# Another order of all engines, with rings of ten and eight buffers, in a fused state-space and local-attention kernel

## The chip, the cores and the metric

The kernel runs on one core of a Trainium2 chip. The metric is the device time of one execution in microseconds, lower is better. The engines are TensorE (PE; PEld is its weight loading), VectorE (DVE), ScalarE (ACT), GpSimd (POOL) and SyncE (SP), which issues all DMAs. Each runs its own instruction stream in order, and the streams meet through semaphores.

## What is computed

From x of 8 sequences x 256 tokens x 128 features, a layer norm gives xn. Two branches start from it:

```python
xn = _layernorm(x)
s = mamba_block(xn)           # projection, causal convolution of 4 taps, silu, softplus,
                              # scan hc = a*hc + b over 256 tokens for 256 x 16 states, output projection
for i in range(6):            # the other branch
    x = attn_layer(shift_tokens(x), Wqkv[i], ...) + x   # 16 heads of 64, windows of 32 that look one window back
    x = ffn_layer(shift_tokens(x), ...) + x             # layer norm, a * gelu(gate), 128 -> 2*341 -> 128
g = silu(x)
out = x0 + s * g              # x0: the kernel's input
```

In attention, q and k are normalised by head, scaled and rotated; the softmax runs over 64 positions of two windows.

## The kernel before

Everything stays in on-chip memory. After a start phase (layer norm, transposes, constants) the main phase treats the attention branch as 48 steps, s = 8 * layer + sequence. A step's attention is cut into eight units of q and k (`qk`, half the tokens x 4 heads; line 623), four of values (`value`, line 639) and four groups of heads (`scores` lines 660 and 668, `values_out` line 702). Its way through the engines:

- TensorE `qk(s,u)` -> ScalarE `square` (line 979) -> VectorE `rotate` (two multiplications, line 1307) and `sum_squares` (line 1314) -> after all eight: `guard_q` (line 1321), ScalarE `guess_q`, VectorE `norm_q` (line 1330).
- GpSimd `rotate_sum` (line 1584, adds the two products into the ring AB of NAB slots) and `normalise` (line 1595) -> TensorE `turn` (four transposes, line 648) -> ScalarE `copy_qk` (line 988).
- TensorE `scores` -> VectorE `softmax` (lines 1337, 1340) -> ScalarE `expo` (line 995) -> VectorE `sum_p` (line 1350) -> GpSimd `normalise_p` (line 1602) -> TensorE `turn_p` (line 680) -> ScalarE `copy_p` (line 1003) -> TensorE `values_out` -> ScalarE `copy_o`.
- For a pair of sequences: `w_out` (line 719), `res_attention`, `mean_x` (line 726), `center` (VectorE, line 1366), `square_x` (ScalarE, sqx), `var_x` (line 732), `norm_x`, `w_gelu` (line 745), `gelu`, `w_gate` (line 758), `gate`, `w_down` (line 767), `res_ff`.

The state-space branch takes one sequence ("batch") every six steps; its operations have names with z_ and are spread over eleven steps. `z_x` (line 776), `z_tap`, `z_conv` (VectorE, line 1403: six shifted multiply-adds, and a small addition), `z_silu`, `z_dbc`, `z_dup` (line 804), `z_softplus`, `z_delta` make its inputs, and `z_g` (line 785) its gate. Then sixteen chunks j of 128 rows each: a DMA spreads rows (`replicate`), ScalarE makes the decay into the single PSUM bank M (`z_decay`, line 1164), GpSimd makes the input product (`z_bu`, line 1629) in the ring hb of NH slots, VectorE scans (`z_scan`, line 1417), GpSimd multiplies by C (`z_hc`, line 1640), and TensorE sums four chunks (`z_sum`, line 822). `z_gate`, `z_out` and `z_state` end the batch.

Each operation is a Python function with its waits inside, and returns at once when its step does not exist, is odd (pair operations) or is not a multiple of six (z_ operations). Every engine's function has one loop, `for i in STEADY` (i from -2 to 46), whose body is a list of calls with lags, as `z_scan(i - 5, 6)`. That hand-written list is the order of that engine: what has lag 5 comes, for a batch that starts at step s, in iteration s + 5. Behind the loops stand lists for the last step and the tail. At the switch to the next layer, `rotate_sum` of units 6 and 7 also makes rotation tables (line 1575), and SP loads the next weights (`next_qk`, `next_v`, `other_weights`).

PSUM banks are shared: the bank of R alternates between `qk`/`value` units, T takes all transposes, X scores and outputs, C0 the pair's work, M the z_ work, Y the sums. Who may write T, X and M after whom is worked out by `befores` from T_ORDER, X_ORDER and M_ORDER (lines 53 to 62), which must repeat TensorE's or ScalarE's order:

```python
            def rotate_sum(s, u):
                ...
                if n >= NAB:
                    pool.wait_ge(tr_full, n - NAB + 1)
...
            def z_bu(s, j):
                ...
                if n >= NH:
                    pool.wait_ge(zy_full, (n - NH) // ZSUM + 1)
```

Of the kernel before, what the change touches and what calls it, by code (L numbers as in the profile page):

```python
# [40 lines left out]
LAST = STEPS - 1  # L41
LAST_B = STEPS - BSTEP
LAST_Z = 16 * (STEPS // BSTEP - 1)
NAB = 9
NREP = 4
NH = 9
# [9 lines left out]
X_ORDER = [("values_out", 3, 1, 1), ("scores", 0, 0, 1), ("scores", 1, 0, 1), ("values_out", 0, 0, 1),  # L56
           ("scores", 2, 0, 1), ("values_out", 1, 0, 1), ("scores", 3, 0, 1), ("values_out", 2, 0, 1)]
M_ORDER = [("z_x", 0, -2, 6), ("z_out", 0, 9, 6), ("z_dbc", 0, 1, 6), ("z_dup", 0, 1, 6), ("z_g", 0, 4, 6),
           ("z_decay", 8, 6, 6), ("z_decay", 14, 8, 6), ("z_decay", 5, 5, 6), ("z_decay", 9, 6, 6),
           ("z_decay", 15, 8, 6), ("z_decay", 3, 4, 6), ("z_decay", 10, 6, 6), ("z_decay", 11, 7, 6),  # L60
           ("z_decay", 4, 4, 6), ("z_decay", 0, 3, 6), ("z_decay", 6, 5, 6), ("z_decay", 1, 3, 6),
           ("z_decay", 12, 7, 6), ("z_decay", 13, 7, 6), ("z_decay", 2, 3, 6), ("z_decay", 7, 5, 6)]
# [240 lines left out]
def main_phase(nc, t, k, R2, T, C0, X, M, Y):  # L303

    with ExitStack() as ctx:
# [142 lines left out]
        def _(sp):  # L448
# [105 lines left out]
            for i in STEADY:  # L554
                replicate(i - 6, 6)
                next_qk(i, 1)
                next_qk(i, 2)
                spread(i, 0)
                replicate(i - 3, 1)
                next_v(i, 0)  # L560
                next_qk(i, 3)
                spread(i, 1)
                replicate_bc(i - 3, 0)
                replicate_bc(i - 3, 1)
                next_qk(i + 1, 0)
                replicate(i - 3, 2)
                replicate_bc(i - 3, 2)
                replicate_bc(i - 3, 3)
                replicate(i - 2, 0)
                replicate(i - 6, 7)  # L570
                spread(i, 2)
                replicate_bc(i - 3, 4)
                spread(i, 3)
                arrange_x(i + 1)
                replicate(i - 5, 5)
                replicate(i - 4, 4)
                replicate(i - 3, 3)
                next_v(i, 1)
# [17 lines left out]
        def _(pe):  # L596
# [1254 lines left out]
```

## Time and profile before

| what | value |
|---|---|
| median of 3 runs | 1792.14 us (1791.08 to 1795.57) |
| profiled execution, its own time | 1786.7 us |
| its span | 1784.9 us |
| TensorE busy | 1691.1 us, 95% |
| VectorE busy | 1555.8 us, 87% |
| GpSimd busy | 1426.6 us, 80% |
| ScalarE busy | 1257.4 us, 70% |
| DMA | 113.13 MB, mean 63 GB/s |

The profile is that of one execution. An engine's busy time is the union of its instructions; ends of matmuls are modelled, and of pipelined ones they overlap the next start. Idle time in front of an instruction is put down to what released it last. In the timeline, rows give start and length in us, engine, line, operation, tiles (out<-in) with their shapes, and how many instructions are merged; idle time before them stands in brackets.

### The profile page before, as it was taken

Reading aid. Unit: us, or ns where it says so; the run is one execution under the profiler, and the core shown is the slowest. Engines: PE = TensorE matmul, PEld = TensorE weight load, DVE = VectorE, ACT = ScalarE, POOL = GpSimd, SP = SyncE. Lnnn points to the kernel's source line nnn. Section 1 sums busy time; section 2 is a strip of 40 time slices with the busy share of each in tenths; the row PEclk is TensorE's granted clock in tenths of the full one; section 3 lists DMA queues with packets and bytes.
Section 4 is the critical chain, followed back from the end, with each engine's and each line's share of the span. In section 5 each row is a group of like instructions: output and inputs, shape, how many; then the busy total and the mean of one; then the engine's idle time right before and its main releaser. Section 6 shows DMA issues by size and latency. Waiting matters only on the chain.

```text
span 1784.9 us, 73875 instructions
## 1 busy us (share of the span) xinstructions
PE 1691.1 (95%) x30944; PEld 983.4 (55%) x30944; DVE 1555.8 (87%) x2724; ACT 1257.4 (70%) x2328; POOL 1426.6 (80%) x1264
## 2 busy tenths in 40 slices
PE   3789999999999999999999999999999999999976
PEld 1355555555555655555555555555555555555542
DVE  5768999889989899899988999898998899989856
ACT  3566686776876777866867768667678677786665
POOL 1677888977888887888889878897888888798862
PEclk9999999999999999999999999999999999999999
DMA  4013233131312422132331423214131332213230
GB/s 112 22 40 72 50 88 81 38 91 44 89 30 55 111 66 47 36 74 69 82 72 26 89 55 75 77 37 94 46 80 29 82 85 64 50 37 69 53 93 24
DMA packets 94054, 113.13 MB, mean 63 GB/s; under 512 B 42318, under 2 KB 59484, under 8 KB 93724
## 3 DMA queue, kind: packets, MB, share of 16 engines
q1 hardware_dynamic: 93724, 108.41, 25.7%
q8 instruction: 246, 4.03, 1.0%
q14 instruction: 84, 0.69, 0.1%
HBM read 19.22 MB, written 1.05 MB: 11 GB/s over the span
## 4 chain that ended last, share of the span: by engine, by line
PE 62%; DVE 15%; POOL 9%; issue 8%; ACT 3%; DMA 1%; SPq 1%; POOLq 0%; DVEq 0%; ACTq 0%
PE bank L623 12%; PE bank L648 8%; PE bank L702 8%; PE bank L639 7%; PE bank L719 6%; PE bank L668 5%; PE bank L680 4%; DVE qn L1307 3%; PE bank L745 3%; DVE qc L1307 3%; POOL AB L1595 2%; POOL AB L1584 2%; PE bank L758 2%; DVE ssq L1314 2%; POOL hb L1629 2%
## 5 line engine op out<-in xcount | busy, mean ns | idle before, releaser
L1584 POOL TENSOR_TENSOR AB<-qc,qn 128x512 f32<-128x512 f32 x384 | 487.0, 1274 | 105.2 <-DVE qn L1307 103.2
L1595 POOL TENSOR_TENSOR AB<-AB,rinv 128x512 f32<-128x512 f32 x384 | 411.4, 1094 | 34.1 <-DVE rinv L1330 34.1
L623 PE MATMUL bank<-wqkv,XT 128*128 128x512 f32 x768 | 381.3, 599 | 5.2 <-DVE qn L1307 5.1
L1602 POOL TENSOR_TENSOR Pb<-Pb,p_rden 128x512 f32<-128x512 f32 x192 | 200.4, 1044 | 139.4 <-DVE p_rden L1351 137.4
L988 ACT ACTIVATE qkT<-bank 128x512 f32<-128x512 f32 x384 | 228.8, 596 | 109.1 <-PE bank L648 107.2
L979 ACT ACTIVATE sq<-bank 128x512 f32<-128x512 f32 x384 | 228.4, 595 | 95.7 <-PE bank L623 95.6
L1314 DVE TENSOR_REDUCE ssq<-sq 128x8 f32<-128x512 f32 x384 | 258.3, 673 | 9.9 <-ACT sq L979 9.2
L1307 DVE TENSOR_TENSOR qc<-bank,rt 128x512 f32<-128x512 f32 x384 | 258.6, 673 | 8.4 <-ACT sq L979 5.4
L1307 DVE TENSOR_TENSOR qn<-bank,rt 128x512 f32<-128x512 f32 x384 | 261.5, 681 | 0.0
L702 PEld LDWEIGHTS bank<-PT,V 64*64 64x64 f32 x12288 | 197.2, 135 | 97.4 <-issue 89.3
L648 PE MATMUL bank<-ident,AB 128*128 128x128 f32 x1536 | 242.7, 281 | 5.3 <-ACT qkT L988 2.7
L648 PEld LDWEIGHTS bank<-ident,AB 128*128 128x128 f32 x1536 | 173.7, 141 | 124.9 <-issue 82.2
L702 PE MATMUL bank<-PT,V 64*64 64x32 f32 x12288 | 218.1, 220 | 7.3 <-ACT PT L1003 3.6
L1003 ACT ACTIVATE PT<-bank 128x512 f32<-128x512 f32 x192 | 114.0, 594 | 153.2 <-PE bank L680 150.7
L639 PE MATMUL bank<-wqkv,XV 128*128 128x512 f32 x384 | 192.4, 603 | 6.0 <-DVE qn L1307 6.0
L1337 DVE TENSOR_REDUCE mx<-bank 128x8 f32<-128x512 f32 x192 | 131.4, 684 | 71.8 <-PE bank L668 71.1
L1417 DVE TENSOR_TENSOR_SCAN hb<-bank,hb 128x256 f32<-128x256 f32 x256 | 161.2, 671 | 29.5 <-ACT bank L1164 29.5
L719 PE MATMUL bank<-OT,wo 128*128 128x512 f32 x384 | 182.1, 597 | 0.0
L1629 POOL TENSOR_TENSOR hb<-rep,BC 128x512 f32<-128x512 f32 x128 | 162.9, 1279 | 17.7 <-PE bank L822 7.9
L623 PEld LDWEIGHTS bank<-wqkv,XT 128*128 128x128 f32 x768 | 127.9, 192 | 79.9 <-issue 70.2
L668 PE MATMUL bank<-qkT 64*32 64x64 f32 x12288 | 164.3, 222 | 2.5 <-issue 2.4
L995 ACT ACTIVATE Pb<-Pb 128x512 f32<-128x512 f32 x192 | 120.8, 629 | 62.5 <-DVE Pb L1340 62.3
(141 smaller groups left out, 2531.5 us busy)
## 6 DMA issues: line engine op xcount, KB each, us to landing
V<-V SPq DMA_DIRECT2D x672, 64.0 KB, 2.0
rep<-du SPq DMA_DIRECT2D x64, 512.0 KB, 4.8
wqkv<-in_Wqkv SPq DMA_DIRECT2D x36, 256.0 KB, 3.3
XV<-XT SPq DMA_DIRECT2D x96, 64.0 KB, 2.1
wo<-in_Wo SPq DMA_DIRECT2D x6, 512.0 KB, 5.3
BC<-BC SPq DMA_DIRECT2D x8, 256.0 KB
w<-in_W SPq DMA_DIRECT2D x6, 341.0 KB, 4.5
BC<-BC SPq DMA_DIRECT2D x8, 128.0 KB
```

The costliest lines, as they stand in the source:

```text
L623: pe.matmul(R[u % 2][:], XT[:, s % NB, (u % 2) * P:(u % 2 + 1) * P], wqkv[:, (u // 2) * 512:(u // 2 + 1) * 512], start=True, stop=True).th ...
L639: pe.matmul(R[n % 2][:], XV[:, q % 2, s % 2, tl, :], wqkv[:, c:c + 512], start=True, stop=True)\
L648: mm = pe.transpose(T[:, c * P:(c + 1) * P], AB[:, (8 * s + u) % NAB, c * P:(c + 1) * P], ident[:])
L668: mm = pe.matmul(SB[w * WIN:(w + 1) * WIN, odd, col:col + 2 * WIN], qkT[p0:p0 + DH, g % 2, c, WIN + tok:2 * WIN + tok], qkT[p0:p0 + DH, g ...
L702: mm = pe.matmul(o_bank(s)[DH * odd:DH * (odd + 1), tl, c * P + w * WIN:c * P + (w + 1) * WIN], V[r, w, h0:h0 + DH], PT[r, g % 2, 2 * odd ...
L719: mm = pe.matmul(c_bank("w_out", s), wo[:, k, :], flat(OT[:, k]), start=k == 0, stop=k == 7)
L979: act.activation(sq[:, u % 2, :], R[u % 2][:], ACT.Square).then_inc(sq_done, 1)
L988: act.activation(qkT[:, g % 2, :, WIN + tl * P:WIN + (tl + 1) * P], T.rearrange("p (c t) -> p c t", c=4), ACT.Copy).then_inc(qkT_done, 1)
L1307: ins = dve.tensor_tensor(out if z == 0 else out[:, :, :, ::-1, :], src, tab, ALU.mult)
L1314: dve.reduce_sum(ssq[:, 8 * u:8 * u + 8], sq[:, u % 2, :].rearrange("p (h d) -> p h d", d=DH), AX_X)\
L1584: pool.tensor_tensor(AB[:, n % NAB, :], qc[:, u % 2, :], qn[:, u % 2, :], ALU.add).then_inc(rs_done, 1)
L1595: pool.tensor_tensor(o, o, r, ALU.mult).then_inc(nm_done, 1)
```

## The change

All five lists of the steady loops are reordered, X_ORDER and M_ORDER with them; NAB goes from 9 to 10 and NH from 9 to 8. No operation's body changes. Some calls change their lag, that is, cross the edge of an iteration: `values_out(·, 3)` 1 to 0, `z_sum(·, 0)` 5 to 4, `z_gate` 9 to 8, `z_silu` -1 to 0, scans 2, 10 and 13 to one more, `z_bu` 3, 10, 11, and `z_hc` 0, 3, 4, 5, 8, `arrange_x` -1 to -2, and `next_qk` 1 to 3 from i to i + 1. Three calls of the last step's lists go, since the loop now makes them. The core of the diff (of SP, ScalarE and GpSimd what the texts speak of):

```diff
-NAB = 9
+NAB = 10
 NREP = 4
-NH = 9
+NH = 8
...
-X_ORDER = [("values_out", 3, 1, 1), ("scores", 0, 0, 1), ("scores", 1, 0, 1), ("values_out", 0, 0, 1),
-           ("scores", 2, 0, 1), ("values_out", 1, 0, 1), ("scores", 3, 0, 1), ("values_out", 2, 0, 1)]
+X_ORDER = [("scores", 0, 0, 1), ("scores", 1, 0, 1), ("values_out", 0, 0, 1), ("scores", 2, 0, 1),
+           ("values_out", 1, 0, 1), ("scores", 3, 0, 1), ("values_out", 2, 0, 1), ("values_out", 3, 0, 1)]
...
@@ SP
+                arrange_x(i + 2)
...
-                arrange_x(i + 1)
...
+                next_qk(i + 1, 1)
+                next_qk(i + 1, 2)
+                next_qk(i + 1, 3)
                 replicate(i - 4, 4)
...
@@ TensorE
             for i in STEADY:
+                turn(i, 0)
                 value(i, 2)
-                turn(i, 0)
-                values_out(i - 1, 3)
                 turn(i, 1)
                 value(i, 3)
                 scores(i, 0)
+                z_x(i + 2)
                 turn(i, 2)
+                z_out(i - 9)
                 qk(i + 1, 0)
-                qk(i + 1, 1)
-                turn(i, 3)
-                z_x(i + 2)
-                z_sum(i - 5, 0)
-                z_out(i - 9)
                 z_dbc(i - 1)
                 w_out(i - 2, 0)
+                turn(i, 3)
+                qk(i + 1, 1)
+                z_g(i - 4)
                 scores(i, 1)
                 turn_p(i, 0)
                 qk(i + 1, 2)
-                w_out(i - 2, 1)
+                turn(i, 4)
                 w_gelu(i - 3, 0)
                 values_out(i, 0)
+                turn(i, 5)
+                qk(i + 1, 3)
                 z_dup(i - 1)
-                turn(i, 4)
-                qk(i + 1, 3)
                 w_gelu(i - 3, 1)
-                turn(i, 5)
                 qk(i + 1, 4)
-                z_g(i - 4)
+                w_gelu(i - 3, 2)
+                w_out(i - 2, 1)
+                scores(i, 2)
+                qk(i + 1, 5)
+                turn_p(i, 1)
                 w_out(i - 2, 2)
-                w_gelu(i - 3, 2)
-                scores(i, 2)
-                turn_p(i, 1)
-                qk(i + 1, 5)
+                w_gate(i - 3, 0)
                 qk(i + 1, 6)
-                w_gate(i - 3, 0)
                 turn(i, 6)
                 values_out(i, 1)
                 turn(i, 7)
+                w_out(i - 2, 3)
                 w_gate(i - 3, 1)
-                w_out(i - 2, 3)
                 qk(i + 1, 7)
-                w_gate(i - 3, 2)
                 scores(i, 3)
                 turn_p(i, 2)
+                w_gate(i - 3, 2)
                 mean_x(i - 2)
                 value(i + 1, 0)
+                z_sum(i - 7, 2)
+                values_out(i, 2)
+                var_x(i - 2)
+                w_down(i - 3)
+                turn_p(i, 3)
                 z_sum(i - 6, 1)
-                w_down(i - 3)
-                z_sum(i - 7, 2)
+                z_sum(i - 4, 0)
                 z_sum(i - 8, 3)
-                var_x(i - 2)
-                values_out(i, 2)
-                turn_p(i, 3)
                 value(i + 1, 1)
+                values_out(i, 3)
...
-            values_out(LAST - 1, 3)
...
-            z_sum(LAST_B, 0)
...
@@ VectorE
             for i in STEADY:
-                z_gate(i - 9)
+                z_scan(i - 7, 10)
+                z_scan(i - 4, 2)
+                z_scan(i - 8, 13)
                 res_ff(i - 4)
                 softmax(i, 0)
-                z_scan(i - 5, 5)
                 z_scan(i - 8, 14)
                 z_scan(i - 6, 8)
+                z_state(i - 9)
+                z_conv(i + 2)
                 sum_p(i, 0)
+                sum_squares(i + 1, 0)
                 rotate(i + 1, 0)
-                sum_squares(i + 1, 0)
-                z_conv(i + 2)
-                z_scan(i - 6, 9)
                 softmax(i, 1)
                 rotate(i + 1, 1)
-                z_scan(i - 8, 15)
+                rotate(i + 1, 2)
                 sum_squares(i + 1, 1)
-                rotate(i + 1, 2)
+                z_scan(i - 3, 0)
+                z_scan(i - 5, 5)
...
                 softmax(i, 3)
                 center(i - 2)
+                gate(i - 3, 2)
+                sum_p(i, 3)
+                sum_squares(i + 1, 6)
                 sum_squares(i + 1, 7)
                 guard_q(i + 1)
-                sum_p(i, 3)
-                z_scan(i - 3, 0)
                 rotate(i + 1, 7)
                 norm_q(i + 1)
-                z_scan(i - 6, 10)
-                z_scan(i - 3, 1)
-                z_scan(i - 5, 6)
-                z_scan(i - 7, 12)
-                z_scan(i - 3, 2)
-                z_scan(i - 7, 13)
                 norm_x(i - 2)
                 z_scan(i - 4, 4)
+                z_scan(i - 5, 6)
+                z_gate(i - 8)
+                z_scan(i - 7, 12)
                 z_scan(i - 5, 7)
+                z_scan(i - 3, 1)
@@ GpSimd
                 normalise(i, 0)
                 normalise(i, 1)
-                z_hc(i - 8, 12)
+                z_hc(i - 6, 4)
+                z_bu(i - 5, 7)
                 normalise(i, 2)
                 normalise(i, 3)
-                z_bu(i - 4, 4)
+                z_hc(i - 7, 9)
+                z_hc(i - 4, 1)
+                z_hc(i - 8, 12)
+                rotate_sum(i, 7)
                 normalise(i, 4)
-                z_bu(i - 7, 11)
+                z_hc(i - 8, 13)
+                normalise_p(i, 0)
+                z_bu(i - 7, 12)
                 normalise(i, 5)
-                z_hc(i - 6, 6)
-                z_hc(i - 5, 3)
-                rotate_sum(i, 7)
-                normalise_p(i, 0)
-                normalise(i, 6)
...
-            z_hc(LAST_B, 3)
```

## Rows read from the trace of the kernel before

**Rows 1.** The page: busy time, share and instructions of each engine.

```profile
PE 1691.1 (95%) x30944; PEld 983.4 (55%) x30944; DVE 1555.8 (87%) x2724; ACT 1257.4 (70%) x2328; POOL 1426.6 (80%) x1264
```

**Rows 2.** The page: the chain that ended last, by engine.

```profile
PE 62%; DVE 15%; POOL 9%; issue 8%; ACT 3%; DMA 1%; SPq 1%; POOLq 0%; DVEq 0%; ACTq 0%
```

**Rows 3.** Stages: window, length, busy of PE, PEld, DVE, ACT, POOL, clock, DMA.

```profile
56.00:188.80 132.80, 118.62 (x2377) 71.19 (x2376) 101.39 (x180) 84.09 (x157) 96.44 (x86) 0.97 0.24 54
188.80:1662.50 1473.70, 1455.06 (x27035) 849.92 (x27034) 1335.90 (x2326) 1083.37 (x2011) 1249.66 (x1099) 1.00 0.27 64
1662.50:1784.90 122.40, 95.24 (x1482) 51.19 (x1480) 82.84 (x136) 70.54 (x130) 68.55 (x59) 0.95 0.21 51
```

**Rows 4.** The same view, the step with the convolution (i mod 6 = 4).

```profile
820.10:857.40 37.30, 35.98 (x646) 21.42 (x644) 34.38 (x64) 24.97 (x52) 30.59 (x29) 1.00 0.17 42
```

**Rows 5.** TensorE's waits: whole span, then 188.8 to 1662.5 (total, times, longest).

```profile
PE bank L732 <- ACT sqx L1037: 8.3, 9, 0.9
...
PE bank L680 <- POOL Pb L1602: 3.5, 6, 0.9
...
PE bank L639 <- DVE qn L1307: 1.6, 6, 0.5
```

**Rows 6.** Timeline of TensorE: stages and what follows them.

```profile
902.17 1.02 PE L623 MATMUL bank<-wqkv,XT 128*128 128x512 f32 x2
902.61 0.14 PEld L648 LDWEIGHTS bank<-ident,AB 128*128 128x128 f32 x1 [0.24 <-issue]
903.03 0.60 PE L648 MATMUL bank<-ident,AB 128*128 128x128 f32 x4
903.47 1.88 PE L719 MATMUL bank<-OT,wo 128*128 128x512 f32 x4
905.28 0.30 PE L660 MATMUL bank<-maskb,identb 64*32 64x256 bf16 x8
...
919.61 0.66 PE L648 MATMUL bank<-ident,AB 128*128 128x128 f32 x4
920.11 1.88 PE L719 MATMUL bank<-OT,wo 128*128 128x512 f32 x4
921.82 1.02 PE L623 MATMUL bank<-wqkv,XT 128*128 128x512 f32 x2
...
733.24 1.12 PE L804 MATMUL bank<-dbc,dupW 16*128 16x256 f32 x4
...
842.53 1.03 PE L785 MATMUL bank<-HT,inW 128*128 128x256 f32 x4
```

**Rows 7.** Timeline, end of a class 4 step: mean, centring, variance, sum_p.

```profile
854.65 1.02 PE L726 MATMUL bank<-XT,mean 128*128 128x512 f32 x2
...
856.07 0.68 DVE L1366 TENSOR_TENSOR xc<-XT,bank 128x512 f32<-128x512 f32 x1
...
857.46 1.12 PE L732 MATMUL bank<-sqx,mean 128*128 128x512 f32 x2 [0.93 <-ACT sqx L1037]
857.49 0.68 DVE L1350 TENSOR_REDUCE p_den<-Pb 128x8 f32<-128x512 f32 x1
```

**Rows 8.** Timeline, a layer's end: normalise_p 0 and turn_p 0.

```profile
870.25 1.03 POOL L1602 TENSOR_TENSOR Pb<-Pb,p_rden 128x512 f32<-128x512 f32 x1
...
871.42 0.63 PE L680 MATMUL bank<-ident,Pb 128*128 128x128 f32 x4 [0.93 <-POOL Pb L1602]
```

**Rows 9.** Timeline: rotate 7, and the value stage that waits for it.

```profile
822.89 0.68 DVE L1307 TENSOR_TENSOR qn<-bank,rt 128x512 f32<-128x512 f32 x1
...
823.63 1.98 PE L639 MATMUL bank<-wqkv,XV 128*128 128x512 f32 x4 [0.32 <-DVE qn L1307]
```

**Rows 10.** Timeline, class 4: rotate 0, convolution, and the qk 2 that follows.

```profile
833.01 0.68 DVE L1307 TENSOR_TENSOR qn<-bank,rt 128x512 f32<-128x512 f32 x1
...
834.20 2.68 DVE L1403 SCALAR_TENSOR_TENSOR x1s<-bank,mvec,x1s 128x255 f32<-128x255 f32 x6
...
836.09 1.02 PE L623 MATMUL bank<-wqkv,XT 128*128 128x512 f32 x2
```

More of the change, by code:

```diff
@@ L1482, in _ @@
                 sum_squares(i + 1, 3)
-                rotate(i + 1, 3)
+                z_scan(i - 6, 9)
                 rotate(i + 1, 4)
+                softmax(i, 2)
                 sum_squares(i + 1, 4)
                 z_scan(i - 4, 3)
-                softmax(i, 2)
+                gate(i - 3, 0)
                 rotate(i + 1, 5)
-                gate(i - 3, 0)
+                sum_p(i, 2)
+                rotate(i + 1, 6)
+                gate(i - 3, 1)
+                z_scan(i - 7, 11)
@@ L1490, in _ @@
                 sum_squares(i + 1, 5)
-                sum_p(i, 2)
-                gate(i - 3, 1)
-                rotate(i + 1, 6)
-                gate(i - 3, 2)
                 res_attention(i - 2)
-                z_scan(i - 7, 11)
-                sum_squares(i + 1, 6)
                 softmax(i, 3)
                 center(i - 2)
+                gate(i - 3, 2)
+                sum_p(i, 3)
+                sum_squares(i + 1, 6)
                 sum_squares(i + 1, 7)
                 guard_q(i + 1)
-                sum_p(i, 3)
@@ L1676, in _ @@
+                z_bu(i - 5, 8)
+                z_bu(i - 7, 13)
                 rotate_sum(i + 1, 2)
                 normalise_p(i, 1)
-                z_hc(i - 7, 8)
-                z_hc(i - 8, 13)
+                normalise(i, 6)
+                normalise(i, 7)
+                z_bu(i - 5, 9)
                 rotate_sum(i + 1, 3)
-                z_bu(i - 4, 6)
+                z_bu(i - 3, 1)
                 rotate_sum(i + 1, 4)
-                z_hc(i - 7, 9)
-                z_bu(i - 3, 0)
+                z_bu(i - 4, 4)
@@ L1685, in _ @@
+                z_bu(i - 7, 14)
+                z_hc(i - 6, 6)
+                z_hc(i - 6, 7)
                 z_hc(i - 7, 10)
-                z_bu(i - 3, 1)
-                z_hc(i - 4, 1)
+                z_bu(i - 4, 5)
+                z_bu(i - 3, 2)
+                normalise_p(i, 2)
+                z_hc(i - 7, 11)
+                z_hc(i - 4, 3)
+                z_hc(i - 3, 0)
+                z_hc(i - 6, 8)
                 rotate_sum(i + 1, 5)
                 z_hc(i - 8, 14)
-                z_hc(i - 6, 7)
@@ L1691, in _ @@
[L1691 to L1694 removed]
                 z_hc(i - 8, 15)
[L1696 to L1697 removed]
+                z_bu(i - 7, 15)
+                normalise_p(i, 3)
+                z_bu(i - 6, 11)
                 rotate_sum(i + 1, 6)
[L1699 to L1703 removed]
@@ L1704, in _ @@
-                z_bu(i - 6, 10)
-                normalise_p(i, 3)
-                z_bu(i - 5, 9)
+                z_bu(i - 4, 6)
+                z_bu(i - 5, 10)
             normalise(LAST, 0)
             normalise(LAST, 1)
-            z_hc(LAST_B, 3)
             normalise(LAST, 2)
```

104 lines of the change are left out of this document (45 added, 59 removed).

## The prediction

> **What bounds the kernel now.** I read the page first. TensorE is busy for 1691.1 of 1784.9 us, 95% [rows 1], and the chain that ended last runs 62% through it and 15% through VectorE [rows 2]. Busy time alone would not say whether TensorE waits for others, since its ends are modelled, so I then cut the span by stages [rows 3]. From 188.8 to 1662.5 us, where seven batches of six steps run, it lacks only 1473.7 - 1455.1 = 18.6 us of being busy all the time, 1.3% of that stretch. The fill before it lacks 132.8 - 118.6 = 14.2, and the tail behind it 122.4 - 95.2 = 27.2, but the tail's order is nearly untouched. So a new order can win about 19 us in the loop and a part of 14 in the fill, and anything that makes TensorE's own work longer costs its full length. The tightest step after TensorE's own is the one that carries the convolution (i mod 6 = 4, "class 4" below): VectorE 34.4 and TensorE 36.0 of 37.3 us [rows 4]. Last I read what TensorE waited for [rows 5]: var_x for its squares (8.3 us in 9 waits, one each batch), turn_p for normalised scores (3.5 in the loop), value for a rotate (1.6).
>
> Counts, not guesses: the matmuls, activations, vector and GpSimd instructions and DMAs are the same in kind and number. NAB and NH change only how early a ring slot is free. With NAB = 10, rotate_sum(i+1, u) needs turn(i, u-2) instead of turn(i, u-1), and no wait of rows 5 is on that. With NH = 8, z_bu j needs the z_sum over state product j-8; the diff puts z_sum 0 at lag 4 before z_bu 8 (lag 5), and z_sum 1 at lag 6 before z_bu 12 (lag 7), at least an iteration's end between them. I cost both at nothing, bounds 0 and, if a z_bu did block GpSimd, the slower case below. On SP's queue, arrange_x goes an iteration earlier, past spreads 2 and 3; values_out 2 stands near the iteration's end, some ten stages after their copies, which covers them. The replicates keep the classes in which they are wanted, and the next_qk loads end sooner. Nothing for that queue either.
>
> **Edit by edit**, TensorE's time in the whole run:
>
> 1. *var_x later.* In class 4 mean_x runs, one value stage covers it, and var_x then waits 0.93 us [rows 7], because VectorE's centring starts at 856.07 and ScalarE's square follows. The new order puts values_out(i, 2) between them, over 1 us of work, which is more than the wait. Takes away up to 8.3 [rows 5]. Late next is turn_p 3: the stages in front of it lose that pause. But VectorE takes sum_p 3 directly after centring instead of behind two other operations (centring ends at 856.75, sum_p starts at 857.49 [rows 7]), 0.7 us earlier. I count -8.3; between 0 and -8.3.
> 2. *normalise_p 0 earlier.* When a layer ends, GpSimd also makes tables, and turn_p 0 waits 0.93 us [rows 8]. Three of the six waits in the loop are of this kind, some 2.6 of the 3.5 us. The new GpSimd order has one fewer normalise (five instead of six) in front of normalise_p 0, and one takes 1.03 like the operation in rows 8. -2.6; between 0 and -3.5.
> 3. *Scan 0 away from rotate 7.* value(i+1, 1) waits for rotate 7 [rows 9], in whose front z_scan(i-3, 0) stood. It moves to mid-iteration. -1.6; between 0 and -1.6, since two sums of squares now stand before rotate 7.
> 4. *TensorE's own seams.* Stages differ in how they join. A transposing stage behind a full matmul shows 0.60 us, behind a small-tile stage (scores, values_out, z_sum) 0.66: 0.06 dearer [rows 6]. A four-matmul projection shows 1.03 behind a full stage and 1.12 behind values_out: I take 0.10, near it, as the price of a full stage behind a small one. A w_out gives way to a qk after 921.82 - 920.11 = 1.71 us, but to scores after 905.28 - 903.47 = 1.81 [rows 6]: 0.10 for each entry into small tiles. Now I count both orders by hand. Transposes behind small stages: 8 each step before (turn 1, 2, 4, 7 and all turn_p), 6 after (turn 0, 2, 5, 7, turn_p 0, 2): 12 x 0.06 = 0.72 less for a batch. Full stages behind small ones: new are qk 5 behind scores 2 in all six steps, w_down behind values_out 2 in three, value 1 behind a z_sum in three: 12 x 0.10 = 1.20 more (var_x paid it already; z_x and z_dup change places). Entries: two extra z_sum entries before, three after: 0.10 more. Sum +0.58 for a batch, x 8 = +4.6.
> 5. *Convolution ahead of sum_p 0 and rotate 0.* Before, rotate 0 ends at 833.01 + 0.68 = 833.69 and the qk that needs it starts at 836.09: slack 2.4 [rows 10]. The convolution, 2.68 + about 0.2, and its wait for the tap, some 0.7 (estimated from z_x starting only after scores 0), go in front: rotate 0 comes 3.6 later. z_g, now ahead of that qk, gives 0.86 back. 3.6 - 2.4 - 0.8 = 0.4 a batch, +3.2; between 0 and 1.2 x 8 = 9.6. What queues behind it on VectorE is softmax 1, which can start no earlier than scores 1 anyway.
>
> The other moves (scans 2, 10, 13 over an iteration's edge, state products, silu, z_gate) stay in the same order against their own producers, with the one M bank passed on equally often; they lie beside TensorE's work, at nothing while item 5's slack lasts.
>
> Sum: -8.3 - 2.6 - 1.6 + 4.6 + 3.2 = -4.7. The profiled execution took 1786.7, so 1782.0; the median of the runs shown, 1792.1, is 5.4 above it, which gives **1787.4**. A difference under 0.3% (5.4 us) can't be told from none here.
>
> **A rule against a row.** Item 4's first price rests on weights loaded early: the load for a turn began at 902.61, while the qk started at 902.17 was still running for 1.02 us, over the same 128 rows [rows 6]. The Trainium skill (TensorE: Matmul & The Clock Gate, "The mechanism" of the part on packing small matmuls) says that a weight load overlaps matmuls in flight only where the row group differs. By that rule no such load is early and seams would cost alike in any order; the sum would be without item 4. The row shows the overlap, so I go by the row.
>
> **Rivals.**
> - *Seams cost the same in total* (their differences are only in the modelled ends, or hidden): without item 4, -9.3, so 1782.8. For it: the prices are 0.06 and 0.10 us, read at few places. Against: the start of the next stage moves with them.
> - *VectorE becomes the bound in class 4* (slower). The convolution in front delays not one qk but all that VectorE owes: item 5 costs 1.2 instead of 0.4 a batch (+6.4 on the sum), and at the step's end centring is as late as before, so the 8.3 of var_x stays: -4.7 + 6.4 + 8.3 = +10.0, 1802. It decides if rotate 0 ends over 0.9 us past the moment at which qk 2 could start. For it: 34.4 of 37.3 us busy [rows 4]. Against: scan 0, which ran between the guard_q that opens this step and the next, now runs earlier.
> - *The waits only move*: half of the 12.5 comes back at turn_p 3 and turn 0, whose chain by guard_q starts two operations later: about +1.5, 1794.
> - *Nearly all of the loop's idle time goes*: -18.6 + 4.6 = -14.0, 1778.
>
> **How the numbers follow.** Forecast 0.40, split between just over and just under the 5.4 us (faster 0.18, same 0.20, slower 0.02). Equal seams 0.18 (faster 0.17, same 0.01). VectorE 0.20 (slower 0.17, same 0.03). Waits move 0.15 (same 0.13, slower 0.02). All idle gone 0.07 (faster). Sum: faster 0.42, same 0.37, slower 0.21. The range, 1775 to 1803, reaches from a little under the last case (some of the fill's 14.2 too) to the slower one.
>
> **What the new profile would show.** Right: no wait of var_x for sqx in class 4; turn_p for Pb under 2 us in the loop; TensorE idle there about 9 instead of 18.6, while its busy time in the loop has grown by some 4; seven six-step periods in a little under their 1473.7 us [rows 3]. L623 behind scores 2 joined 0.10 worse. Wrong: a new large wait of qk, value or turn for VectorE or GpSimd in class 4; GpSimd waiting for Y or hb; those periods more than 7 us longer in sum; or gains in the fill or the tail, which I leave at nothing.

## The result and the profile after

The changed kernel takes 1832.47 us, the median of four runs (1830.94 to 1840.32), beside 1791.61 (1785.98 to 1795.57) for the kernel before on the same chip: 1.0241 times as long (95% interval 1.0223 to 1.0258; the two medians alone give 1.0228), 40.9 us slower. The prediction, 1787.4 in a range of 1775 to 1803, was wrong in size and in sign. The profiled execution has a span of 1829.1 against 1784.9, 44.2 us more.

The page of the changed kernel, its engines and its chain, which answer to [rows 1, 2]:

```profile
PE 1716.3 (94%) x30944; PEld 982.3 (54%) x30944; DVE 1587.7 (87%) x2724; ACT 1245.5 (68%) x2328; POOL 1422.4 (78%) x1264
...
POOL 42%; issue 23%; PE 22%; DVE 5%; DMA 2%; SPq 2%; ACT 2%; POOLq 0%; DVEq 0%; ACTq 0%
```

The instructions are as many as before. TensorE is busy for 25.2 us more and VectorE for 31.9 more, with the same work. The chain that ran 62% through TensorE now runs 42% through GpSimd, an engine that is idle for a fifth of the time. I took that as a sign that something holds others at its operations, not that it is full.

To place the loss I cut each span at the 4th and the 46th guard_q, which encloses seven whole batches in every kernel. The windows of the kernel before, then of the changed one (window, length, busy of PE, PEld, DVE, ACT, POOL, clock, DMA; the first window is the end of the fill):

```profile
56.00:155.60 99.60, 86.34 (x1744) 51.94 (x1742) 72.54 (x132) 58.82 (x113) 68.69 (x62) 0.97 0.16 38
155.60:1629.18 1473.58, 1454.02 (x27030) 849.18 (x27030) 1335.04 (x2323) 1083.23 (x2011) 1250.07 (x1098) 1.00 0.27 64
```

```profile
56.00:163.10 107.10, 95.29 (x1810) 56.16 (x1810) 76.27 (x135) 62.24 (x116) 68.68 (x63) 0.90 0.20 44
163.10:1671.30 1508.20, 1468.93 (x27023) 843.30 (x27022) 1363.07 (x2323) 1071.81 (x2009) 1246.56 (x1099) 1.00 0.27 63
```

The seven batches take 1508.2 instead of 1473.6 us, 34.6 more; the fill takes 7.5 more (163.1 against 155.6) and the tail 2.1 more (1829.1 - 1671.3 against 1784.9 - 1629.2). The 34.6 have two parts: TensorE's idle time doubled (1508.2 - 1468.9 = 39.3 instead of 19.6), and its busy time grew by 14.9. VectorE is busy for 28.0 us more in the same stretch with the same 2323 operations.

What TensorE waits for in the seven batches of the changed kernel (total, times, longest), to be held against [rows 5]:

```profile
PE bank L639 <- DVE qn L1305: 21.7, 31, 1.8
PE bank L660 <- ACT qkT L986: 7.8, 8, 1.2
PE bank L623 <- DVE qn L1305: 4.2, 3, 1.7
PE bank L680 <- POOL Pb L1600: 3.9, 15, 1.0
```

The waits of var_x (line 732) are gone, as forecast. In their place value 1 (line 639) waits for rotate 7, 31 times in the 42 steps, 21.7 us instead of 1.6. And one VectorE operation has changed its length. Line 1319 is guard_q, in the kernel before line 1321 (duration ns, least/median/most); first before, then after:

```profile
L1321 DVE TENSOR_SCALAR ssc<-ssq x48: 195/196/771, 58.1 to 1699.1; 128x64 f32<-128x64 f32 x48
```

```profile
L1319 DVE TENSOR_SCALAR ssc<-ssq x48: 194/1220/1228, 57.8 to 1741.9; 128x64 f32<-128x64 f32 x48
...
  ACT lnq L1027: 61.6, 41
```

The same instruction on the same 64 columns has a median of 1.22 us instead of 0.20, and guess_q waits for it 41 times. The timeline of one step (start, length, engine, line, in brackets the idle time before) shows why:

```profile
914.99 1.23 DVE L1312 TENSOR_REDUCE ssq<-sq 128x8 f32<-128x512 f32 x2
...
915.15 1.04 POOL L1600 TENSOR_TENSOR Pb<-Pb,p_rden 128x512 f32<-128x512 f32 x1 [3.40 <-DVE p_rden L1349]
...
916.15 1.26 POOL L1582 TENSOR_TENSOR AB<-qc,qn 128x512 f32<-128x512 f32 x1
...
916.25 1.21 DVE L1319 TENSOR_SCALAR ssc<-ssq 128x64 f32<-128x64 f32 x1
...
917.38 0.68 DVE L1305 TENSOR_TENSOR qc<-bank,rt 128x512 f32<-128x512 f32 x1
917.49 0.26 ACT L1027 ACTIVATE lnq<-ssc 128x64 f32<-128x64 f32 x1 [1.56 <-DVE ssc L1319]
...
917.98 0.67 DVE L1305 TENSOR_TENSOR qn<-bank,rt 128x512 f32<-128x512 f32 x1
...
918.71 1.12 PE L639 MATMUL bank<-wqkv,XV 128*128 128x512 f32 x2 [0.23 <-DVE qn L1305]
```

Read it from the top. sum_p 3 stands ahead of the two last sums of squares now, so normalise_p 3 starts on GpSimd at 915.15 and leaves that engine free at 916.2, where it goes on with rotate_sum 6 (916.15, 1.26 us). guard_q starts 0.10 later, at 916.25, and ends at 917.46, 0.05 after GpSimd's operation (917.41). Rotate 7, behind it on VectorE, ends a microsecond late, and value 1 waits for that. The order now puts every engine into the same place in every round, so guard_q is held in 40 of the 48 steps: 33 times by rotate_sum 6, as here, and 7 times by a z_bu. In the kernel before, guard_q was stretched in 11 steps, each time by a z_bu and to 0.77 us at most. In a typical step it ran while GpSimd waited for p_rden:

```profile
857.38 0.20 DVE L1321 TENSOR_SCALAR ssc<-ssq 128x64 f32<-128x64 f32 x1
...
858.48 1.04 POOL L1602 TENSOR_TENSOR Pb<-Pb,p_rden 128x512 f32<-128x512 f32 x1 [2.76 <-DVE p_rden L1351]
```

The Trainium skill (SBUF — State Buffer, "Who interferes with whom") has the rule for this: VectorE in a two-port mode, which tensor_scalar can enter, shares a pair of ports with GpSimd, whoever issues first holds it for its whole instruction, and the other is blocked. The trace agrees: 1.22 instead of 0.20 us, and in all 40 steps the end comes 0.05 to 0.06 us behind the end of a GpSimd operation. The mode itself is no row of a trace.

### The profile page after: what moved, and what is told of

Its sections match the earlier page's. It is cut to its first block, busy times and chain, and to the rows that moved or that the text cites. A ratio compares the mean times of both kernels' runs of the same rounds, so it can differ in the third digit from the quotient of the medians.

```text
span 1829.1 us, 73875 instructions
## 1 busy us (share of the span) xinstructions
PE 1716.3 (94%) x30944; PEld 982.3 (54%) x30944; DVE 1587.7 (87%) x2724; ACT 1245.5 (68%) x2328; POOL 1422.4 (78%) x1264
## 4 chain that ended last, share of the span: by engine, by line
POOL 42%; issue 23%; PE 22%; DVE 5%; DMA 2%; SPq 2%; ACT 2%; POOLq 0%; DVEq 0%; ACTq 0%
POOL AB L1582 16%; POOL AB L1593 11%; POOL hb L1638 6%; POOL hb L1627 5%; PE bank L623 4%; POOL Pb L1600 3%; PE bank L648 3%; PE bank L702 3%; PE bank L719 2%; PE bank L639 2%; DMA BC<-BC 2%; PE bank L668 1%; PE bank L745 1%; SPq L462 1%; PE bank L680 1%
## 5 line engine op out<-in xcount | busy, mean ns | idle before, releaser
L1582 POOL TENSOR_TENSOR AB<-qc,qn 128x512 f32<-128x512 f32 x384 | 489.3, 1282 | 20.7 <-DVE qn L1305 20.1
L1593 POOL TENSOR_TENSOR AB<-AB,rinv 128x512 f32<-128x512 f32 x384 | 405.9, 1076 | 45.0 <-DVE rinv L1328 45.0
L623 PE MATMUL bank<-wqkv,XT 128*128 128x512 f32 x768 | 399.9, 608 | 11.2 <-DVE qn L1305 11.2
L648 PE MATMUL bank<-ident,AB 128*128 128x128 f32 x1536 | 247.6, 284 | 4.4 <-ACT qkT L986 2.1
L1312 DVE TENSOR_REDUCE ssq<-sq 128x8 f32<-128x512 f32 x384 | 248.5, 665 | 0.1
L639 PE MATMUL bank<-wqkv,XV 128*128 128x512 f32 x384 | 206.0, 619 | 29.9 <-DVE qn L1305 29.5
L1638 POOL TENSOR_TENSOR hb<-hb,BC 128x512 f32<-128x512 f32 x124 | 160.9, 1303 | 14.2 <-DVE hb L1415 14.2
```

Of the source, the lines that this page charges most:

```text
L623: pe.matmul(R[u % 2][:], XT[:, s % NB, (u % 2) * P:(u % 2 + 1) * P], wqkv[:, (u // 2) * 512:(u // 2 + 1) * 512], start=True, stop=True).th ...
L639: pe.matmul(R[n % 2][:], XV[:, q % 2, s % 2, tl, :], wqkv[:, c:c + 512], start=True, stop=True)\
L648: mm = pe.transpose(T[:, c * P:(c + 1) * P], AB[:, (8 * s + u) % NAB, c * P:(c + 1) * P], ident[:])
L1312: dve.reduce_sum(ssq[:, 8 * u:8 * u + 8], sq[:, u % 2, :].rearrange("p (h d) -> p h d", d=DH), AX_X)\
L1582: pool.tensor_tensor(AB[:, n % NAB, :], qc[:, u % 2, :], qn[:, u % 2, :], ALU.add).then_inc(rs_done, 1)
L1593: pool.tensor_tensor(o, o, r, ALU.mult).then_inc(nm_done, 1)
```

## The experiments

The theory that they test: the block of guard_q costs most of the 41 us, and sum_p 3 ahead of it is what brings it about. The rivals: the order itself (guard_q late behind sum_p 3), the rings, or TensorE's new order.

### The reduction: a guard_q that can't be blocked

The same result by another instruction: each sum stands beside 1e-24 in a pair, and a maximum over pairs takes the place of the comparison with a scalar. (sum_squares writes every second element, and GpSimd fills in the constants once, at the start.) Otherwise e1 is the changed kernel and e6 the kernel before.

```diff
-        ssq = m.sb("ssq", [P, 64])
+        ssq = m.sb("ssq", [P, 64, 2])
...
-                dve.tensor_scalar(ssc[:], ssq[:], 1e-24, None, ALU.max).then_inc(ssc_done, 1)
+                dve.reduce_max(ssc[:], ssq[:], AX_X).then_inc(ssc_done, 1)
```

> The new kernel with one instruction in another form: guard_q takes the maximum with 1e-24 by a reduction over pairs (sum of squares, 1e-24) instead of by TENSOR_SCALAR; every order stays. Lock theory (the TENSOR_SCALAR waits until the GpSimd operation that began before it has ended, in 40 of 48 steps, 1.02 us each): guard_q takes 0.2 to 0.3 us everywhere, the waits of value 1 for rotate 7 nearly vanish, 1790 to 1797 us. Order theory (sum_p 3 and two sums of squares in front of guard_q make rotate 7 late by their own 1.5 us, whatever guard_q takes): 1820 to 1832 us.

> The kernel before with guard_q as a reduction over pairs. Its 15 or so partly blocked guard_q (0.3 to 0.77 us instead of 0.2) become 0.29 us, the other 33 get 0.09 us longer: the two cancel on VectorE's time; lock theory and the price of the form both give 1788 to 1796 us. It is the base against which e1_new_reduce (1804.1) has to be read.

e1: 1804.11 us, ratio 1.0068 (1.0046 to 1.0091). e6: 1788.09, ratio 0.9992 (0.9978 to 1.0006), the same as before. e1's guard_q and its seven batches:

```profile
L1319 DVE TENSOR_REDUCE ssc<-ssq x48: 285/286/288, 59.4 to 1716.0; 128x64 f32<-128x128 f32 x48
```

```profile
161.04:1645.88 1484.84, 1466.11 (x27023) 842.38 (x27022) 1348.31 (x2323) 1073.99 (x2009) 1246.49 (x1099) 1.00 0.27 64
```

All 48 take 0.286 us, though 47 of them start while a GpSimd operation runs, and the kernel is 28.4 us faster (1832.5 - 1804.1), though each guard_q is 0.09 longer in itself. TensorE's idle time in the seven batches falls from 39.3 to 18.7, what it was before (19.6). So the block is worth 28 of the 41 us. The expectation for a block alone, 1790 to 1797 us, was missed by 7, so there is a rest. In the old order, where guard_q is stretched in 11 steps and by 0.58 us at most, the same edit changes nothing. The same page of the Trainium skill says that tensor_reduce never contends on trn2; these runs agree.

What is left, 1804.1 - 1788.1 = 16.0 us between e1 and e6, is hardly idle time in the loop: 18.7 against 17.9. TensorE's busy time there is 13.1 longer, 1466.1 against 1453.0. (The two profiled spans differ by 20.3: 14.0 in the seven batches, 3.6 in the fill and 2.7 in the tail.)

### The order of guard_q and sum_p 3

e2 is the changed kernel with sum_p 3 behind guard_q. e3 is the kernel before with guard_q late.

```diff
@@ e2, in the changed kernel's VectorE loop
-                sum_p(i, 3)
                 sum_squares(i + 1, 6)
                 sum_squares(i + 1, 7)
                 guard_q(i + 1)
+                sum_p(i, 3)
                 rotate(i + 1, 7)
@@ e3, in the VectorE loop of the kernel before
-                sum_squares(i + 1, 6)
                 softmax(i, 3)
                 center(i - 2)
+                sum_p(i, 3)
+                sum_squares(i + 1, 6)
                 sum_squares(i + 1, 7)
                 guard_q(i + 1)
-                sum_p(i, 3)
                 z_scan(i - 3, 0)
```

> The new kernel with sum_p(i, 3) moved behind guard_q on VectorE, the rest of the new order kept. Both theories give the time back: guard_q finds GpSimd idle and comes 0.9 us earlier: 1788 to 1800 us. If it stays over 1815, the loss is neither of the two but elsewhere in the new order (rings, SP queue, seams of TensorE).

> The kernel before with the new order's tail on VectorE alone: softmax 3, center, sum_p 3, sum_squares 6 and 7, guard_q. GpSimd's order stays the old one, in which nothing but normalise_p 3 (and in one step of six a z_bu) follows before normalise(i+1, 0). Lock theory: guard_q starts 0.16 us after normalise_p has ended, so it stays near 0.2 us in five of six steps: 1790 to 1802 us. Order theory: the full loss, 1820 to 1832 us.

e2: 1836.45 us, 1.0257 (1.0231 to 1.0284). e3: 1820.72, 1.0173 (1.0147 to 1.0198). Neither went as expected: both theories had e2 give the time back, and it gives nothing, and e3 lands where the order alone was expected to put it. In e2 guard_q is free (0.195 in every step), but turn_p 3 waits for normalise_p 3, and rinv, an operation with two inputs, is stretched to a median of 1.18 us. e2's wait of TensorE in the loop, and its rinv:

```profile
PE bank L680 <- POOL Pb L1600: 30.7, 31, 1.6
```

```profile
L1328 DVE SCALAR_TENSOR_TENSOR rinv<-tq,yq x48: 226/1177/1196, 58.7 to 1749.1; 128x64 f32<-128x64 f32 x48
```

In e3 guard_q is blocked in 7 of 48 steps, and value 1 waits all the same, for a rotate 7 that comes late. So in the kernel before, this order of VectorE costs some 29 us nearly without a block (1820.7 against 1791.5). The same two views of e3, with guard_q's row:

```profile
PE bank L639 <- DVE qn L1307: 16.9, 15, 1.3
```

```profile
L1321 DVE TENSOR_SCALAR ssc<-ssq x48: 195/195/1221, 57.5 to 1724.5; 128x64 f32<-128x64 f32 x48
```

So the two kernels want opposite orders: the new TensorE order needs sum_p 3 early (e2), the old one needs guard_q early (e3). That each TensorE order hides the other's delay is my reading, which no run tests by itself.

### Making the block in the kernel before

e4 is e3 with rotate_sum 6 moved behind normalise_p 3 on GpSimd, the neighbour that it has in the changed kernel; e5 is e4 with the reduction.

```diff
@@ GpSimd
-                rotate_sum(i + 1, 6)
                 z_hc(i - 7, 11)
...
                 normalise_p(i, 3)
+                rotate_sum(i + 1, 6)
                 z_bu(i - 5, 9)
```

> The same as e3_old_guard_late, and on GpSimd rotate_sum(i+1, 6) moved to right behind normalise_p(i, 3), as the new order has it. Lock theory: guard_q now meets a 1.27 us GpSimd operation that began just before it, in all steps: some 1.2 us per guard_q and 1825 to 1840 us. Order theory: as e3_old_guard_late, within 5 us.

> e4_old_late_collide with guard_q as a reduction over pairs, as in e1_new_reduce; nothing else. Lock theory: all of the 48 us between e4_old_late_collide (1868.5) and e3_old_guard_late (1820.7) goes, and the 8 collisions that e3_old_guard_late had as well, less 0.09 us per guard_q for the longer form: 1812 to 1822 us. Rival (moving rotate_sum 6 behind normalise_p 3 costs by itself, by making rotate_sum late): it stays over 1850.

e4: 1868.48 us, 1.0427 (1.0406 to 1.0448). e5: 1823.15, 1.0197 (1.0180 to 1.0214). e4's guard_q, and what value 1 waits for:

```profile
L1321 DVE TENSOR_SCALAR ssc<-ssq x48: 195/1221/1297, 58.0 to 1776.3; 128x64 f32<-128x64 f32 x48
```

```profile
PE bank L639 <- DVE qn L1307: 46.4, 41, 2.3
```

The block can be made at will: with GpSimd's operation put beside it, guard_q is blocked in 46 of 48 steps, again with a median of 1.22 us, and 48 us are added to e3. The reduction takes 45 of them back (1868.5 - 1823.2), about 1 us for each blocked step. e5 stays 2.4 above e3 although e3 still has 7 blocked steps and e5 none, so moving rotate_sum 6 probably costs a few us by itself. (e4 lies 28 us above the range expected of it, and e5 1 us above its own.) Together with e1 and e6 this shows cause and size in both orders.

### The rings

e7 is the changed kernel with NAB = 9 and NH = 9, as before.

```diff
-NAB = 10
+NAB = 9
-NH = 8
+NH = 9
```

> The new kernel with nine slots in both rings, as before, and nothing else changed. If the rings do nothing, as the prediction has it: 1828 to 1837 us (the new kernel 1832.5). If ten slots for rotated rows are needed by the new order: over 1840; if eight for the state products cost: under 1825.

1836.59 us (1832.44 to 1840.69), 1.0270 (1.0247 to 1.0292), beside 1.0241 (1.0223 to 1.0258) with ten and eight. The intervals overlap: the rings do nothing that can be told, as forecast. guard_q is blocked in 40 steps here too.

### The predicted gains, each alone in the kernel before

e9 puts values_out 2 ahead of var_x (item 1), e10 moves scan 0 behind rotate 7 and norm_q (item 3), and e11 does both, with the reduction.

```diff
@@ e9, TensorE
-                var_x(i - 2)
                 values_out(i, 2)
+                var_x(i - 2)
                 turn_p(i, 3)
@@ e10, VectorE
-                z_scan(i - 3, 0)
                 rotate(i + 1, 7)
                 norm_q(i + 1)
+                z_scan(i - 3, 0)
```

> The kernel before with one move on TensorE, the prediction's item 1 alone: var_x(i - 2) behind values_out(i, 2). If item 1 holds: var_x's waits for sqx (8.3 us in 9) go, turn_p 3 waits no more than before: 1781 to 1785 us against 1790.3. Rival (turn_p 3 only loses its cover, since in this order sum_p 3 still stands behind guard_q): its waits for normalised scores grow by as much, 1788 to 1793 us.

> The kernel before with the prediction's item 3 alone: z_scan(i - 3, 0) behind norm_q instead of in front of rotate 7 on VectorE. If item 3 holds: value's waits for rotate 7 in the loop (1.6 us) go, and normalise 0 starts 1.2 us earlier in eight steps: 1787 to 1790 us. Rival: the wait is replaced by one for z_decay 1 or 2, whose bank M comes free later: no difference that can be told.

> e9_old_var_later and e10_old_scan0_later together, and guard_q as a reduction over pairs, to see whether there is a kernel faster than both. If the gains add up: 1778 to 1784 us; if they replace one another: 1786 to 1791.

e9: 1794.02 us, 1.0020 (1.0006 to 1.0034). e10: 1797.65, 1.0031 (1.0017 to 1.0045). e11: 1799.04, 1.0046 (1.0031 to 1.0061). None gains; each is a little slower, and e10 and e11 lie above every range expected for them. In the profiles the seven batches take 4.9 us more in e9 and in e10 than before (1478.5 against 1473.6). TensorE's waits in e9's loop, then in e10's:

```profile
PE bank L680 <- POOL Pb L1602: 11.6, 16, 1.0
PE bank L648 <- ACT PT L1003: 3.3, 12, 0.3
```

```profile
PE bank L732 <- ACT sqx L1037: 7.3, 8, 0.9
PE bank L680 <- POOL Pb L1602: 4.5, 7, 0.9
PE bank L648 <- ACT qkT L988: 3.9, 7, 0.6
PE bank L648 <- ACT PT L1003: 3.0, 7, 0.7
```

In e9 the 7.4 us of var_x in these batches are gone, and turn_p waits 8.1 more (11.6 instead of 3.5) and turn 3.3 for the copy of PT. That is the rival "the waits only move", and more than the half that it spoke of. But e9 leaves VectorE's order alone, while the change also brings sum_p 3 forward, and there turn_p waits only 3.9. So e9 shows item 1 without its helper. In e10 the 1.6 of value 1 are gone, and turn waits 6.9 for ScalarE; the change puts scan 0 into another place than e10 does.

### TensorE's seams

e8 is e1 with another order at the step's end and turn_p 1 ahead of qk 5; e12 is e1 with the second of these alone.

```diff
@@ e8 and e12
                 scores(i, 2)
-                qk(i + 1, 5)
                 turn_p(i, 1)
+                qk(i + 1, 5)
@@ e8 alone: the step's end, in this order
+                w_down(i - 3)
+                z_sum(i - 6, 1)
+                z_sum(i - 7, 2)
+                z_sum(i - 4, 0)
+                z_sum(i - 8, 3)
+                var_x(i - 2)
+                values_out(i, 2)
+                turn_p(i, 3)
+                value(i + 1, 1)
```

> e1_new_reduce (1804.1) with TensorE's seams put back where they were: turn_p 1 directly behind scores 2 and in front of qk 5; and at the step's end w_down, all z_sum, var_x, values_out 2, turn_p 3, value 1, values_out 3. Seam theory (the new order makes TensorE's own work some 1.1 us longer for a batch, by full matmul stages behind small-tile ones and by more entries into these): TensorE's time in seven batches without its gaps is shorter by 5 to 9 us; 1794 to 1803 us, if var_x's old wait (0.9 us a batch) does not come back, and up to 1808 if it does. Rival (the 12.7 us left over the kernel before are waits, not seams): no change of that time.

> e1_new_reduce (1804.1) with one seam put back: turn_p(i, 1) directly behind scores(i, 2), then qk(i + 1, 5). Seam theory, with the joints read in the traces (qk 0.96 behind scores and turn_p 0.44 behind qk, against turn_p 0.49 and qk 0.86): 0.05 us a step, 2.3 us: 1800 to 1804, and the three stages together take 0.05 us less where nothing waits. Rival (turn_p 1 needed the cover of qk 5, since normalise_p 1 comes late in this order): its waits grow by more than that, over 1806.

e8: 1854.77 us, 1.0376 (1.0356 to 1.0396), far above its expectation, since values_out waited 22.9 us for the copies of PT. Its TensorE is busy for 1478.6 us in the seven batches, 12.4 more than in e1, where 5 to 9 less were expected, although the records show fewer full stages at a dear seam. So busy time holds more than seams, and e8 can't price them. e12: 1801.60, 1.0063 (1.0044 to 1.0082), beside e1's 1.0068 (1.0046 to 1.0091): not to be told apart by the times, but the records can tell. The groups of TensorE in the seven batches (line, form, count, busy us, mean ns, idle before): the kernel before, then e1, then e12's two that differ.

```profile
L623 PE MATMUL bank<-wqkv,XT 128*128 128x512 f32 x672 | 330.1, 593 | 0.0
L648 PE MATMUL bank<-ident,AB 128*128 128x128 f32 x1344 | 212.1, 280 | 1.1 <-POOL AB L1595 1.1
L680 PE MATMUL bank<-ident,Pb 128*128 128x128 f32 x672 | 108.9, 285 | 5.1 <-POOL Pb L1602 3.5
L745 PE MATMUL bank<-xc,w 128*128 128x512 f32 (+1 forms) x126 | 65.7, 603 | 0.0
L767 PE MATMUL bank<-ge,w 128*128 128x512 f32 (+1 forms) x126 | 57.6, 592 | 0.0
```

```profile
L623 PE MATMUL bank<-wqkv,XT 128*128 128x512 f32 x672 | 346.9, 603 | 4.2 <-DVE qn L1305 4.1
L648 PE MATMUL bank<-ident,AB 128*128 128x128 f32 x1344 | 213.7, 282 | 7.0 <-POOL AB L1594 6.5 <-ACT qkT L986 0.2
L680 PE MATMUL bank<-ident,Pb 128*128 128x128 f32 x672 | 106.0, 280 | 4.1 <-POOL Pb L1601 4.0
L745 PE MATMUL bank<-xc,w 128*128 128x512 f32 (+1 forms) x126 | 68.0, 622 | 0.0
L767 PE MATMUL bank<-ge,w 128*128 128x512 f32 (+1 forms) x126 | 59.7, 610 | 0.0
```

```profile
L623 PE MATMUL bank<-wqkv,XT 128*128 128x512 f32 x672 | 342.2, 596 | 0.0
...
L680 PE MATMUL bank<-ident,Pb 128*128 128x128 f32 x672 | 107.6, 282 | 8.5 <-POOL Pb L1601 7.6
```

The first full matmul of a stage takes 593 ns at some seams (cheap) and 697 at others (dear). Counted in the records of these batches, 71 full ones are dear before and 189 in e1: 118 more by 0.104 us are 12.3. Of the transposes 309 are dear before (0.058 us each) and 284 in e1, 1.5 less. Together 10.8 of the 12.1 us by which TensorE's work grew (1466.1 - 1454.0). e12's one swap takes 7 ns from 672 qk matmuls, 4.7 us, and gives 1.6 to turn_p; its busy time in the loop is 1462.6, 3.5 less than e1's. So seams are real time.

But not every dear one comes from the order of stages. Some start 0.05 us behind the end of the operation that they wait for, and show no idle time because the modelled end of the stage ahead covers it. Two from e1: qk 2 behind rotate 0, and turn 1 behind ScalarE's copy of turn 0:

```profile
209.07 0.68 DVE L1305 TENSOR_TENSOR qn<-bank,rt 128x512 f32<-128x512 f32 x1
209.28 0.63 PE L680 MATMUL bank<-ident,Pb 128*128 128x128 f32 x4
...
209.81 1.12 PE L623 MATMUL bank<-wqkv,XT 128*128 128x512 f32 x2
```

```profile
165.40 0.60 ACT L986 ACTIVATE qkT<-bank 128x512 f32<-128x512 f32 x1 [0.23 <-PE bank L648]
...
166.06 0.65 PE L648 MATMUL bank<-ident,AB 128*128 128x128 f32 x4
```

Rotate 0 ends at 209.75 and qk starts at 209.81. By the records of the seven batches, such short waits are 53 of e1's dear full stages (35 of w_gelu for gelu, 18 of qk) and 38 of those before, and 72 of its dear transposes against 29. Without these, and without the few behind visible idle time (4 in e1, 14 before), the new order has 100 to 110 dear full stages more and some 70 dear transposes fewer than before, which is 6 to 8 us; another 3 or so are the dear starts of short waits. Both are estimates from the counts and the two prices, and they leave 1 to 3 of the 12.1 open. e3 shows the same from the other side: with TensorE's list untouched its busy time is 8.2 us longer than before (1462.2 against 1454.0).

### Is the stretch of norm_q the rest?

In e1 norm_q, whose two operations have two inputs each, is still stretched: the first takes 0.60 us on average instead of 0.22, in 21 of 48 steps (the second 0.24). e13 (from e1), e14 (from e2) and e15 (from e6) put one-input maxima over single elements in their place. They leave out the last refinement of the inverse root with its factor of -2 for q and for k, so the logits are a fourth.

```diff
-                link(dve.tensor_tensor(tq[:], ssc[:], yq2[:], ALU.mult))
+                link(dve.reduce_max(tq[:], yq2[:].rearrange("p (h o) -> p h o", o=1), AX_X))
...
-                dve.scalar_tensor_tensor(rinv[:], tq[:], 3.0, yq[:], ALU.subtract, ALU.mult).then_inc(rinv_done, 1)
+                dve.reduce_max(rinv[:], yq[:].rearrange("p (h o) -> p h o", o=1), AX_X).then_inc(rinv_done, 1)
```

> e1_new_reduce with norm_q's two operations as reductions over one tile each, in the same number, chain and place (it leaves out the Newton step of the inverse root, and the two factors of -2 with it, so the logits are a fourth). If two-input operations blocked by GpSimd (18 us on VectorE over 48 steps) reach the end: turn's waits for normalise (6.5 us) vanish and it takes 1792 to 1800 us. If the rest is TensorE's own work: 1800 to 1805, with its gaps in seven batches smaller by at most 6 us.

> e2_new_guard_first (1836.5) with the same two operations as reductions over one tile (the Newton step is left out), guard_q unchanged. If e2's loss is the lock, moved from guard_q to norm_q (44 us of stretching): 1795 to 1808 us. If it is turn_p 3 waiting for normalise_p 3, which now starts after guard_q (30.5 us of waits): 1820 to 1836, with those waits unchanged.

> e6_old_reduce (1788.1) with the same two operations as reductions over one tile (the Newton step is left out). The kernel before has only some 7 us of stretching in them, mostly where nothing waits: 1783 to 1790 us. It is the base for the other two.

e13: 1814.57 us, 1.0131 (1.0115 to 1.0146). e14: 1837.85, 1.0265 (1.0250 to 1.0280). e15: 1787.96, 0.9992 (0.9982 to 1.0001). e13 is slower than both of its expectations, so its time alone settles nothing; the stretches answer. They are gone (no one-input maximum takes over 0.22 us), and the loop is no shorter. So the stretch of norm_q is no part of the loss there: e14 equals e2 (it is 2 us above its range), and turn_p 3 waits for normalise_p 3 as long as there (30.3 us), so the stretched rinv isn't what holds it. e13's seven batches take 1484.7 us, e1's 1484.8; the wait of turn for normalised rows (6.5) falls to 2.1 and that of scores for the copies of q and k rises from 2.5 to 9.2. The 5.1 us by which e13's profiled span is longer (1809.1 against 1804.0) lie in the tail (163.1 against 158.1), where TensorE's granted clock is 0.59 from 20 to 40 us behind the last guard_q and 0.82 after that, and in e1 0.70 and 0.91. Its median is 10 above e1's; whether the clock did that in its other executions too isn't shown.

## Why the prediction was wrong, point by point

**What bounds the kernel** was read rightly: TensorE, with 19 us of idle time in the loop. But the views that I read rank waits that exist. The rows of guard_q were not among them, and they held the warning: 0.196 us in the median and 0.77 at most, an instruction whose length depends on its neighbour.

**The step that failed** stands in item 3: "two sums of squares now stand before rotate 7". I counted what stands in front of rotate 7 and left out how long guard_q, also in front of it, would take where it now stands. Forecast was -1.6; value's waits grew by 20.1 in the loop. No rival named it either. The slower one was VectorE as the bound in class 4, while guard_q is blocked in five classes of six. One listed sign of being wrong did come, a large wait of value for VectorE with the periods over 7 us longer, but not for the reason given there. The Trainium skill's rule on the shared ports (SBUF — State Buffer) is the one that spoke against this change; the prediction weighed another page's rule.

**Item 1** (var_x, -8.3): the wait went, as forecast. Late next was to be turn_p 3, set at nothing because sum_p 3 starts earlier. In the changed kernel that held: turn_p waits 3.9 us in the loop. Without that help, in e9, turn_p 3 and turn inherit the wait and it is 3.9 us slower. What the early sum_p 3 brought with it, the late guard_q, is the cost that the item left out. Even with a free guard_q the gain doesn't stay: e1 idles as long as the kernel before (18.7 against 19.6), with 6.5 us of turn for normalised rows and 4.1 of qk in place of var_x's 7.4.

**Item 2** (normalise_p 0, -2.6): turn_p's waits in the loop are 3.9 instead of 3.5 [rows 5]. No gain.

**Item 3** without the block: the wait is 0.8 instead of 1.6 us in e1. e10, the scan alone but put behind norm_q, is 7.5 us slower; turn takes up the wait.

**Item 4** (seams, +4.6, of which 4.1 in seven batches): right in kind and too small. TensorE's busy time grew by 12.1 us with free guards (e1), of which 6 to 8 are seams of the order by the estimate above. Full stages at a dear seam were forecast at 84 more (12 a batch), and e1 has 118: the forecast ones (42 for qk 5, 21 for w_down, 20 for value 1) are there at 0.104 each, and beside them came 28 of w_gelu, 20 of qk behind turn_p, 7 of z_x and 3 others, less 19 of w_gate and 4 of value behind turn_p. The transposes were to save 84 dear seams, and saved 25: 42 are dear behind a value stage, a pair that I had counted as cheap, and all 42 start 0.05 us behind ScalarE's copy. They are short waits, which the prediction had nowhere. The rule weighed there, of the Trainium skill (TensorE: Matmul & The Clock Gate, "The mechanism"), would make all seams equal as I applied it. They differ by 0.104 us in the records, so the row holds. I had left out that the same section also lets a load go ahead into a background weight buffer.

**Item 5** (convolution, +3.2): the loop has three visible waits of qk for a rotate, 4.2 us in all, but each comes some 23 us ahead of a convolution, so they are not the forecast one. That one is short and hidden in busy time. In e1, 18 of 42 times qk 2 starts just behind rotate 0, mostly 0.07 us later than else and 0.10 dearer, about 3 us in the loop (an estimate), in three of a batch's six steps. The size is as forecast by luck, since the convolution stands in only one of them.

**Rings and SP's queue** at nothing: e7 agrees for the rings; no run tests SP's queue by itself.

So of the 40.9 us some 28 are the block (e1), and 12 to 16 remain without it (e1 against before and e6). Most of these are TensorE's longer busy time in the loop, 12 to 13 us, which is seams and short waits in shares that are only estimated. The rest lies in the fill and the tail and is shown only in part (last section). None of the kernels run here beats the kernel before; e6 and e15 equal it.

## What to carry to other kernels

A reordering can't be priced by counts and waits alone: ask of every short VectorE operation ahead of a critical one what GpSimd will run beside it in the new order, since an in-order schedule repeats the meeting in every round (1.0 us, 40 times). An operation whose most is far above its median in the old profile marks the place, and a one-input reduction can be a form that is never held (0.286 us in all 48 steps). Test each hoped-for gain alone in the old kernel: both that were tested here only handed their wait on there. And hold TensorE's busy time against a kernel with the same list, since a stage that starts just behind the end of its wait shows no idle time at all.

## What the runs showed of the hardware

**The block has a sharp shape.** guard_q takes 0.195 us free and 1.22 blocked, and it ends 0.05 us behind GpSimd's operation. An operation with two inputs is stretched too (rinv, 0.226 to 1.18 in e2), while the one-input maxima in its place never were (0.22 us at most in e14).

**TensorE's clock in the fill and the tail.** In the seven batches the kernels have a granted clock of 1.00, e4 and e7 of 0.99. Fill and tail differ. e9's tail holds the same work as the tail before, and took 161.2 us instead of 155.7. Windows of the kernel before, then of e9, at the same distance from the last guard_q:

```profile
1709.00:1714.00 5.00, 2.66 (x84) 1.81 (x82) 3.62 (x7) 3.28 (x7) 3.10 (x4) 1.00 0.34 82
1714.00:1719.00 5.00, 3.69 (x148) 3.08 (x148) 2.49 (x5) 3.53 (x7) 3.70 (x5) 1.00 0.51 108
```

```profile
1714.30:1719.30 5.00, 2.80 (x83) 2.19 (x84) 3.58 (x7) 3.18 (x6) 3.00 (x4) 0.92 0.35 82
1719.30:1724.30 5.00, 3.62 (x51) 2.49 (x51) 2.14 (x5) 2.31 (x4) 2.78 (x4) 0.50 0.49 105
```

TensorE had been busy for 2.7 to 2.8 of 5 us in both; behind that the clock stayed at 2.4 GHz in one and was at 1.2 GHz in the other, where 3.6 us of busy time carried 51 instructions instead of 148 in 3.7. What let it fall in one of them isn't shown. The changed kernel's fill shows the same, with a clock of 0.50 from 128 to 133 us where the kernel before has 1.00 (its fill was 7.5 us longer). e9's tail is 5.5 us longer, though its edit is to the loop; how much of that is the clock isn't shown. Single profiled spans shouldn't be compared more finely than that unless the loop is cut out.
